# Two sums with x go from TensorE to VectorE at the end of a delta-rule and expert kernel

## The chip, the cores and the metric

The kernel runs on one core of one Trainium2 chip. The metric is the device time of one launch in microseconds (us). A core has TensorE (PE in the profile), VectorE (DVE), ScalarE (ACT), GpSimd (POOL) and SyncE (SP), which here only issues DMAs. TensorE multiplies out of SBUF into PSUM banks; GpSimd works on SBUF alone in this kernel.

## The reference

The input x is 2 sequences of 2048 tokens of width 256. It is normalised, and from the result two things are made: s, the output of a delta-rule attention with 4 heads, and g, the silu of a top-1 mixture of 8 experts. The output is x + s * g.

```python
xn = layernorm(x)
# s: delta rule, per head; q, k, v, beta are products with xn
def step(S, inp):
    q_t, k_t, v_t, b_t = inp
    pred = einsum('bhk,bhkv->bhv', k_t, S)
    delta = (v_t - pred) * b_t[..., None]
    S = S + k_t[..., :, None] * delta[..., None, :]
    return S, einsum('bhk,bhkv->bhv', q_t, S)
o = o * rsqrt(mean(o * o, -1) + EPS) * norm_w
o = o * (g_attn * sigmoid(g_attn))
s = o.reshape(b, n, H * DV) @ Wo
# g: each token goes through the one expert that its router chose
h = square(relu(einsum('btd,edh->ebth', xn, expert_fc)))
g = silu(sum over e of one_hot * einsum('ebth,edh->ebtd', h, expert_proj))
return x + s * g
```

## The kernel before, in words

The tokens are cut into 16 chunks of 128 tokens for both sequences, numbered 0 to 15. Each engine has its own list of steps, written out by hand: `ramp()`, a loop of `step3` and `step2`, and `tail()`. An engine runs its list strictly in that order; a step first waits on the semaphores of what it needs. So an early step that waits holds up everything behind it on that engine, and nothing on another engine unless that one waits for it.

The experts' part works on 39 tiles of sorted tokens. Its rows are scattered into a DRAM buffer `y_d` and, when all are there, loaded back into `wts` in four DMAs; the view of it for chunk c is `chunk_of(c)`. The output of chunk c is then made in place in two operations:

- `weigh(c)` on VectorE (L1839) multiplies `chunk_of(c)` by s, which lies in the buffer of `xT`.
- The sum with x is made in one of two ways. On TensorE, `add_x(c)` (L733 and L735) multiplies x and the chunk by the identity into one PSUM bank, and `keep_sum(c)` on ScalarE (L1225) copies the bank back. On VectorE, `add_x(c)` (L1844) is one addition. The list `ON_PE` names the chunks of the first kind.

SyncE then sends the 16 chunks out, strictly in the order 0 to 15 (L395), each once its sum is there.

The attention of the last chunk, 15, ends in a chain through four engines: `oss_(15)` and `og_(15)` on VectorE (L1816, L1810), `orn_(15)` and `ogm(15)` on GpSimd (L2424, L2426 and L2432), which scale `og` and signal `og_ok`; `ogT_(15)`, four transposes on TensorE (L710), that wait for `og_ok`; `ogTc(15)` on ScalarE (L1216), which copies them out of PSUM; `wo(15)` on TensorE (L722), the product with Wo, which needs that copy; `s_cp(15)` on ScalarE (L1221); and then `weigh(15)`, `add_x(15)` on VectorE and the last output DMA. These are the ends of the lists of TensorE and of VectorE, with the sums of the chunks put between the links.

```python
def added(c):
    return sum(1 for n in range(c + 1) if (n in ON_PE) == (c in ON_PE))
...
for c in range(NCH):
    sp.wait_ge(out_act if c in ON_PE else out_dve, added(c))
    sp.dma_start(o_v[c], chunk_of(c)).then_inc(o_out, 16)
```

Of the kernel before, what the change touches and what calls it, by code (L numbers as in the profile page):

```python
# [66 lines left out]
def build_program(nc, x, wq, wk, wvg, wbr, wo, norm_w, fc, pj, out):  # L67
    with ExitStack() as ctx:
# [203 lines left out]
        rank_ps = psum[RANK_BANK][:, 0:NQ * E]  # L272
        rows_ps = psum[LG_BANK][:, 0:2 * NT].rearrange("p (z j) -> p z j", z=2)

        ON_PE = [0, 2, 4, 6, 8, 9, 10, 11]

        def added(c):

            return sum(1 for n in range(c + 1) if (n in ON_PE) == (c in ON_PE))

        def sum_bank(c):
            return psum[H_BANK[added(c) % 2]][:].rearrange("p (b d) -> p b d", b=B)
# [31 lines left out]
        def chunk_of(c):  # L314
            return yf[:, c].rearrange("p (b d) -> p b d", b=B)

        def x_of(c):
            return (x_first[:, c] if c < NCH // 2 else x_last[:, c - NCH // 2]).rearrange("p (b d) -> p b d", b=B)
# [4 lines left out]
        with nc.Block() as block:  # L323
            @block.sync
            def _(sp):
# [67 lines left out]
# [3 lines that stand above are left out]
# [3 lines left out]
            def _(pe):  # L399
# [303 lines left out]
                def ogT_(c):  # L703
                    ch = At(pe, c)
                    ch.on(og_ok)
                    if c + 1 < NCH:
                        ch.stage(3, 0, S_ok)
                    for b in range(B):
                        for k in range(KC):
                            ins = pe.transpose(psum[CH_BANK][:, (b * KC + k) * P:(b * KC + k + 1) * P],  # L710
                                               og[:, H * b + 2 * k:H * b + 2 * k + 2, :].rearrange("p h n -> p (h n)"),
                                               ident[:])
                    ins.then_inc(ogTp, 1)
# [12 lines left out]
                def add_x(c):  # L726
                    n = added(c)
                    if n == 1:
                        At(pe, NT - 1).on(y_ok)
                    if n > 2:  # L730
                        pe.wait_ge(out_act, n - 2)
                    pe.wait_ge(xf_in[c // (NCH // 2)], 16 * B * GROUPS // 2)
                    pe.matmul(sum_bank(c), ident[:], x_of(c), start=True, stop=False)  # L733
                    pe.wait_ge(ys_ok, c + 1)
                    pe.matmul(sum_bank(c), ident[:], chunk_of(c), start=False, stop=True).then_inc(sum_ok, 1)  # L735
# [211 lines left out]
                def tail():  # L947
# [141 lines left out]
                    add_x(6)  # L1089
                    add_x(8)  # L1090
                    add_x(9)
                    add_x(10)
                    ogT_(15)
                    add_x(11)
                    wo(15)

                ramp()
# [4 lines left out]
            def _(act):  # L1102
# [40 lines left out]
                def relu(j, n):  # L1143
                    At(act, j).on(hp[n])
                    act.activation(half(n), psum[H_BANK[j % 2 ^ n]][:], ACT.Relu).then_inc(relu_ok[n], 1)  # L1145
# [20 lines left out]
                def ksq_(a, b):  # L1166
                    fr = At(act, a)
                    fr.on(Kp[b])
                    fr.on(Pl_ok[b], back=1)
                    act.activation(h4(f32_t, b), bank4(KG_BANK[b]), ACT.Square).then_inc(ksq[b], 1)  # L1170
# [52 lines left out]
                def keep_sum(c):  # L1223
                    act.wait_ge(sum_ok, SUM_FROM + added(c))
                    act.copy(chunk_of(c), sum_bank(c)).then_inc(out_act, 1)  # L1225
# [186 lines left out]
                def tail():  # L1412
                    ksq_(14, 0)
                    M0c(13, 1)
                    M0c(13, 0)
                    ksq_(14, 1)
                    osq(12)
                    relu(34, 0)
                    sq(34, 0)
                    q_h(14, 0)  # L1420
                    relu(34, 1)
                    sq(34, 1)
                    dZ(13, 0, 0)
                    dZ(13, 0, 1)
                    keep_rows(35)
                    dZ(13, 1, 0)
                    dZ(13, 1, 1)
                    keep_y(34)
                    q_h(14, 1)
                    dZ(13, 2, 0)  # L1430
                    dZ(13, 2, 1)
                    relu(35, 0)
                    sq(35, 0)
                    ogTc(12)
                    kTc(14, 1)
                    kTc(14, 0)
                    dZ(13, 3, 0)
                    dZ(13, 3, 1)
                    sig(14, 0)
                    relu(35, 1)  # L1440
                    sq(35, 1)
                    y_sigmoid(34)
                    dZ(13, 4, 0)
                    dZ(13, 4, 1)
                    s_cp(12)
                    keep_rows(36)
                    dZ(13, 5, 0)
                    dZ(13, 5, 1)
                    keep_y(35)
                    dZf_(13, 0)  # L1450
                    dZf_(13, 1)
                    sig(14, 1)
                    ksq_(15, 0)
                    ksq_(15, 1)
                    relu(36, 0)
                    M0c(14, 0)
                    M0c(14, 1)
                    osq(13)
                    sq(36, 0)
                    q_h(15, 0)  # L1460
                    relu(36, 1)
                    dZ(14, 0, 0)
                    sq(36, 1)
                    dZ(14, 0, 1)
                    kTc(15, 1)
                    dZ(14, 1, 0)
                    dZ(14, 1, 1)
                    keep_rows(37)
                    keep_y(36)
                    kTc(15, 0)  # L1470
                    q_h(15, 1)
                    relu(37, 0)
                    y_sigmoid(35)
                    dZ(14, 2, 1)
                    dZ(14, 2, 0)
                    sq(37, 0)
                    relu(37, 1)
                    ogTc(13)
                    dZ(14, 3, 0)
                    dZ(14, 3, 1)  # L1480
                    sq(37, 1)
                    M0c(15, 0)
                    M0c(15, 1)
                    keep_rows(38)
                    s_cp(13)
                    dZ(14, 4, 0)
                    dZ(14, 4, 1)
                    keep_y(37)
                    relu(38, 0)
                    y_sigmoid(36)  # L1490
                    dZ(15, 0, 0)
                    dZ(15, 0, 1)
                    sq(38, 0)
                    dZ(14, 5, 0)
                    y_sigmoid(37)
                    dZ(14, 5, 1)
                    dZ(15, 1, 1)
                    dZ(15, 1, 0)
                    relu(38, 1)
                    dZf_(14, 0)  # L1500
                    sig(15, 0)
                    dZf_(14, 1)
                    sq(38, 1)
                    dZ(15, 2, 1)
                    dZ(15, 2, 0)
                    keep_y(38)
                    y_sigmoid(38)
                    osq(14)
                    dZ(15, 3, 0)
                    dZ(15, 3, 1)  # L1510
                    sig(15, 1)
                    dZ(15, 4, 0)
                    dZ(15, 4, 1)
                    ogTc(14)
                    s_cp(14)
                    dZ(15, 5, 0)
                    dZ(15, 5, 1)
                    keep_sum(0)
                    dZf_(15, 0)
                    dZf_(15, 1)  # L1520
                    keep_sum(2)
                    osq(15)
                    keep_sum(4)
                    keep_sum(6)
                    keep_sum(8)
                    keep_sum(9)
                    keep_sum(10)
                    ogTc(15)
                    keep_sum(11)
                    s_cp(15)  # L1530

                ramp()
# [4 lines left out]
            def _(dve):  # L1537
# [296 lines left out]
                def weigh(c):  # L1834

                    dve.wait_ge(yf_in[c // CG], 16)
                    At(dve, c).on(s_ok)
                    y = chunk_of(c)
                    dve.tensor_tensor(y, y, s_all[:, 2 * c:2 * c + 2, :], ALU.mult).then_inc(ys_ok, 1)  # L1839

                def add_x(c):
                    dve.wait_ge(ys_ok, c + 1)
                    dve.wait_ge(xf_in[c // (NCH // 2)], 16 * B * GROUPS // 2)
                    dve.tensor_tensor(chunk_of(c), chunk_of(c), x_of(c), ALU.add).then_inc(out_dve, 1)  # L1844
# [232 lines left out]
                def tail():  # L2077
# [180 lines left out]
                    weigh(10)  # L2258
                    add_x(7)
                    weigh(11)  # L2260
                    weigh(12)
                    weigh(13)
                    add_x(12)
                    weigh(14)
# [334 lines left out]
```

## Time and profile before

| | |
|---|---|
| Time, median of 3 runs | 796.43 us (795.91 to 798.44) |
| The profiled execution | 795.13 us, with a span of 793.1 us and 2.03 us around it |
| Busy share of the span | PE 97%, PE weight load 82%, DVE 67%, POOL 49%, ACT 44% |
| Granted TensorE clock | 0.996 on average |

The span runs from the first to the last instruction that the profiler saw. A busy TensorE is not a TensorE at its peak. What the shares say is an average over 793 us; the change is in the last 16 us, and that stretch has its own limits.

### The profile page before, as it was taken

Reading aid. Unit: us, or ns where it says so; the run is one execution under the profiler, and the core shown is the slowest. Engines: PE = TensorE matmul, PEld = TensorE weight load, DVE = VectorE, ACT = ScalarE, POOL = GpSimd, SP = SyncE. Lnnn points to the kernel's source line nnn. Section 1 sums busy time; section 2 is a strip of 40 time slices with the busy share of each in tenths; the row PEclk is TensorE's granted clock in tenths of the full one; section 3 lists DMA queues with packets and bytes.
Section 4 is the critical chain, followed back from the end, with each engine's and each line's share of the span. In section 5 each row is a group of like instructions: output and inputs, shape, how many; then the busy total and the mean of one; then the engine's idle time right before and its main releaser. Section 6 shows DMA issues by size and latency. Waiting matters only on the chain.

```text
span 793.1 us, 22201 instructions
## 1 busy us (share of the span) xinstructions
PE 769.4 (97%) x9002; PEld 649.5 (82%) x9002; DVE 527.5 (67%) x1151; ACT 349.3 (44%) x762; POOL 389.7 (49%) x407
## 2 busy tenths in 40 slices
PE   6988999999999999999999999999999999999987
PEld 5957988888888888889888887888788887879854
DVE  6695475575655657556575667776777767777786
ACT  4713534454444543445344453444444444435432
POOL 3815363553635436354463546546463646545341
PEclk9999999999999999999999999999999999999999
DMA  8508832533335433363333632414142323323075
GB/s 298 195 27 335 330 141 114 196 138 147 128 114 206 151 124 127 114 240 121 120 127 124 229 115 86 156 30 175 45 138 104 128 108 127 128 107 114 9 248 197
DMA packets 37748, 116.25 MB, mean 147 GB/s; under 512 B 3664, under 2 KB 24400, under 8 KB 27664
## 3 DMA queue, kind: packets, MB, share of 16 engines
q1 hardware_dynamic: 33904, 104.62, 36.2%
q0 software_dynamic: 3744, 10.23, 3.9%
q8 instruction: 72, 1.18, 0.6%
q14 instruction: 28, 0.23, 0.1%
HBM read 101.33 MB, written 13.50 MB: 145 GB/s over the span
## 4 chain that ended last, share of the span: by engine, by line
PE 78%; DVE 8%; POOL 6%; issue 4%; DMA 3%; SPq 0%; ACT 0%; DVEq 0%; POOLq 0%
PE bank L504 18%; PE bank L515 16%; PE bank L548 6%; PE bank L533 5%; PE bank L580 5%; PE bank L478 3%; PE bank L480 3%; PE bank L479 3%; PE bank L620 2%; PE bank L722 2%; PE bank L638 2%; PE bank L629 2%; POOL XTl L2398 2%; PE bank L560 2%; POOL ImM L2418 2%
## 5 line engine op out<-in xcount | busy, mean ns | idle before, releaser
L515 PE MATMUL bank<-wts,hT 128*128 128x256 f32 x624 | 170.9, 393 | 0.0
L504 PE MATMUL bank<-xsT,wts 128*128 128x128 f32 x1248 | 166.0, 281 | 0.4 <-ACT xsT L1154 0.3
L504 PEld LDWEIGHTS bank<-xsT,wts 128*128 128x128 f32 x1248 | 150.5, 192 | 11.2 <-issue 11.1
L1761 DVE TENSOR_TENSOR Pm<-bank,lvl_mask 128x256 f16<-128x256 f32 x180 | 68.2, 418 | 67.1 <-PE bank L620 66.3
L515 PEld LDWEIGHTS bank<-wts,hT 128*128 128x128 f32 x624 | 105.4, 191 | 7.3
L2398 POOL TENSOR_TENSOR XTl<-f_t,XTh 128x512 f16<-128x512 f32 x32 | 39.9, 1253 | 137.0 <-DVE XTh L1701 136.9
L1772 DVE TENSOR_TENSOR M<-bank,M 128x256 f16<-128x256 f32 x180 | 68.8, 418 | 53.7 <-PE bank L629 53.2
L1200 ACT CAST Z<-bank 128x256 f16<-128x256 f32 x180 | 59.3, 376 | 99.9 <-PE bank L638 99.8
L1145 ACT ACTIVATE hT<-bank 128x512 f32<-128x512 f32 x78 | 46.7, 599 | 49.1 <-PE bank L504 49.1
L548 PE MATMUL bank<-xT,wq_sb 128*128 128x128 f32 x512 | 63.3, 277 | 0.4 <-DVE qT16l L1706 0.4
L580 PE MATMUL bank<-wvg_sb,xT 128*128 128x512 f32 x128 | 63.2, 617 | 0.0
L533 PE MATMUL bank<-wk_sb,xT 128*128 128x512 f32 x128 | 62.3, 613 | 0.3 <-ACT xT L1119 0.3
L548 PEld LDWEIGHTS bank<-xT,wq_sb 128*128 128x128 f32 x512 | 60.2, 192 | 0.9 <-issue 0.5
L2418 POOL TENSOR_TENSOR ImM<-ident,M 128x512 f32<-128x512 f16 x30 | 35.1, 1188 | 42.6 <-DVE M L1772 42.6
L1149 ACT ACTIVATE hT<-hT 128x512 f32<-128x512 f32 x78 | 49.4, 633 | 1.1
L2392 POOL TENSOR_TENSOR k16l<-f_t,k16h 128x512 f16<-128x512 f32 x32 | 37.9, 1199 | 22.3 <-DVE k16h L1687 22.3
L2371 POOL TENSOR_TENSOR y_sb<-y_sb,y_sg 128x256 f32<-128x256 f32 x39 | 29.5, 757 | 39.3 <-ACT y_sg L1164 39.2
L629 PEld LDWEIGHTS bank<-Pm,Z 128*128 128x128 f16 x720 | 32.8, 98 | 18.3 <-issue 11.4
L1694 DVE TENSOR_TENSOR f_t<-bank,up_neg 128x512 f32<-128x512 f32 x32 | 21.9, 685 | 37.8 <-PE bank L480 37.8
L2375 POOL DMA_INDIRECT y_d<-y_sb,to_row x39 | 41.0, 1052 | 8.6 <-issue 5.5
L2362 POOL DMA_INDIRECT xs<-xn_d,from_row x39 | 40.4, 1035 | 6.8 <-issue 5.9
L2349 POOL TENSOR_TENSOR root<-beta,up_half 128x8 f32<-128x8 f32 x16 | 29.3, 1829 | 29.1 <-DVE gate L1720 16.8
(247 smaller groups left out, 1956.4 us busy)
## 6 DMA issues: line engine op xcount, KB each, us to landing
wts<-in_fc SPq DMA_DIRECT2D x39, 1024.0 KB, 4.9
wts<-in_pj SPq DMA_DIRECT2D x39, 1024.0 KB, 8.1
wts<-in_x SPq DMA_DIRECT2D x10, 512.0 KB, 7.2
wts<-y_d SPq DMA_DIRECT2D x4, 1024.0 KB, 9.5
out_x<-wts SPq DMA_DIRECT2D x16, 256.0 KB, 2.3
xn_d<-wts SPq DMA_DIRECT2D x3, 1024.0 KB, 5.0
x_first<-in_x SPq DMA_DIRECT2D x4, 512.0 KB, 17.6
wts<-in_x SPq DMA_DIRECT2D x4, 256.0 KB, 3.5
```

The lines of the kernel that those rows point to most:

```text
L504: ins = pe.matmul(psum[bank[n]][:, (c % 4) * P:(c % 4 + 1) * P], fcw[r][:, k, c * P:(c + 1) * P], xsT[:, k, :], start=(k == 0), stop=(k == ...
L515: ins = pe.matmul(psum[bank[0]][:, 0:D], hT[:, c, :], pjw[r][:, c, :], start=(c == 0), stop=(c == HC - 1))
L533: ins = pe.matmul(psum[KG_BANK[b]][:], xT[:, a, b, k, :], wk_sb[:, k, :], start=(k == 0), stop=(k == KC - 1))
L548: ins = pe.matmul(bank4(QV_BANK)[:, h, :], wq_sb[:, k, h * DK:(h + 1) * DK], xT[:, a, b, k, :], start=(k == 0), stop=(k == KC - 1))
L580: ins = pe.matmul(psum[QV_BANK][:], xT[:, a, b, k, :], wvg_sb[:, k, :], start=(k == 0), stop=(k == KC - 1))
L629: ins = pe.matmul(half4(level_bank(m, b))[:, h, :], Zs[last(m)][:, H * b + h, :], Pms[last(m)][:, H * b + h, :], start=True, stop=True)
L1149: act.activation(half(n), half(n), ACT.Square).then_inc(sq_ok[n], 1)
L1200: act.copy(evens(h4(Zs[last(m)], b), s, 1), half4(level_bank(m, b)).rearrange("p h (n c) -> p h n c", c=s)).then_inc((last_dZ_ok if last(m ...
L1761: dve.tensor_tensor(h4(Pms[last(m)], b).rearrange("p h (n c) -> p h n c", c=s), half4(level_bank(m, b)).rearrange("p h (n c) -> p h n c", ...
L1772: dve.tensor_tensor(evens(h4(Ms[last(m)], b), s), half4(level_bank(m, b)).rearrange("p h (n c) -> p h n c", c=s), evens(h4(Ms[last(m)], b) ...
L2398: pool.tensor_tensor(h4(XT[1][a % 2], b), h4(f32_t, b), h4(XT[0][a % 2], b), ALU.subtract).then_inc(Xl_ok[b], 1)
L2418: pool.tensor_tensor(h4(ImM, b), ident16[:].unsqueeze(1).to_broadcast([P, H, P]), h4(Ms[last(m)], b), ALU.subtract).then_inc(ImM_ok[b], 1)
```

## The change

`ON_PE` loses chunks 10 and 11. On TensorE the two pairs of products for them go, one from ahead of `ogT_(15)` and one from between `ogT_(15)` and `wo(15)`; on ScalarE the two copies go; on VectorE two additions come in, the one behind `weigh(11)`, the other behind `weigh(12)`. SyncE's list is the same but for the semaphore on which chunks 10 and 11 wait.

```diff
-        ON_PE = [0, 2, 4, 6, 8, 9, 10, 11]
+        ON_PE = [0, 2, 4, 6, 8, 9]
...
                     add_x(9)
-                    add_x(10)
                     ogT_(15)
-                    add_x(11)
                     wo(15)
...
                     keep_sum(9)
-                    keep_sum(10)
                     ogTc(15)
-                    keep_sum(11)
                     s_cp(15)
...
                     weigh(11)
+                    add_x(10)
                     weigh(12)
+                    add_x(11)
                     weigh(13)
```

TensorE, the end of its list, before. L733 and L735 are the two products of one sum (`ident` is the identity), L710 the transposes, L722 the output product:

```order
L733 MATMUL bank<-wts,ident 128x512
L735 MATMUL bank<-wts,ident 128x512
L733 MATMUL bank<-wts,ident 128x512
L735 MATMUL bank<-wts,ident 128x512
L710 MATMUL bank<-ident,og 128x128 x4
L733 MATMUL bank<-wts,ident 128x512
L735 MATMUL bank<-wts,ident 128x512
L722 MATMUL bank<-wo_sb,ogT 128x256 x4
```

TensorE, the same place of the changed kernel:

```order
L733 MATMUL bank<-wts,ident 128x512
L735 MATMUL bank<-wts,ident 128x512
L710 MATMUL bank<-ident,og 128x128 x4
L722 MATMUL bank<-wo_sb,ogT 128x256 x4
```

One sum fewer stands ahead of the transposes, and nothing is left between them and the output product.

VectorE, the end of its list from `og_(15)` (L1810) on, before. L1839 is a `weigh`, L1844 an `add_x`:

```order
L1810 TENSOR_TENSOR og<-bank,gate 128x512
L1839 TENSOR_TENSOR wts<-wts,xT 128x512
L1844 TENSOR_TENSOR wts<-wts,x_first 128x512
L1839 TENSOR_TENSOR wts<-wts,xT 128x512 x3
L1844 TENSOR_TENSOR wts<-wts 128x512
L1839 TENSOR_TENSOR wts<-wts,xT 128x512
L1844 TENSOR_TENSOR wts<-wts 128x512 x2
L1839 TENSOR_TENSOR wts<-wts,xT 128x512
L1844 TENSOR_TENSOR wts<-wts 128x512
```

VectorE, the same place of the changed kernel, where every line number is 4 lower (L1806 is `og_(15)`, L1835 a `weigh`, L1840 an `add_x`):

```order
L1806 TENSOR_TENSOR og<-bank,gate 128x512
L1835 TENSOR_TENSOR wts<-wts,xT 128x512
L1840 TENSOR_TENSOR wts<-wts,x_first 128x512
L1835 TENSOR_TENSOR wts<-wts,xT 128x512
L1840 TENSOR_TENSOR wts<-wts 128x512
L1835 TENSOR_TENSOR wts<-wts,xT 128x512
L1840 TENSOR_TENSOR wts<-wts 128x512
L1835 TENSOR_TENSOR wts<-wts,xT 128x512
L1840 TENSOR_TENSOR wts<-wts 128x512
L1835 TENSOR_TENSOR wts<-wts,xT 128x512
L1840 TENSOR_TENSOR wts<-wts 128x512 x2
L1835 TENSOR_TENSOR wts<-wts,xT 128x512
L1840 TENSOR_TENSOR wts<-wts 128x512
```

Between `og_(15)` and the last `weigh` there are two more additions, and all else stands in the same order.

## Rows read from the trace of the kernel before

**Rows 1.** The page's head and its busy time by engine.

```profile
span 793.1 us, 22201 instructions
PE 769.4 (97%) x9002; PEld 649.5 (82%) x9002; DVE 527.5 (67%) x1151; ACT 349.3 (44%) x762; POOL 389.7 (49%) x407
```

**Rows 2.** The chain that ended last, from 784 us: start, us, what.

```profile
784.46 0.44 PE bank L710 x4
...
786.62 1.74 PE bank L722 x8
...
788.38 0.59 ACT xT L1221
...
789.07 0.70 DVE wts L1839
...
789.79 0.69 DVE wts L1844
```

**Rows 3.** SyncE's issues of output chunks 11 and 15.

```profile
787.26 0.37 SPq L395 DMA_DIRECT2D out_x<-wts  x1
...
790.51 0.37 SPq L395 DMA_DIRECT2D out_x<-wts  x1
```

**Rows 4.** Timeline of TensorE: start, us, engine, line, op [idle before].

```profile
782.58 1.02 PE L733 MATMUL bank<-wts,ident 128*128 128x512 f32 x2
...
784.30 0.60 PE L710 MATMUL bank<-ident,og 128*128 128x128 f32 x4
784.73 1.02 PE L733 MATMUL bank<-wts,ident 128*128 128x512 f32 x2
...
786.45 1.89 PE L722 MATMUL bank<-wo_sb,ogT 128*128 128x256 f32 x8
```

**Rows 5.** Timeline of GpSimd and of ScalarE ahead of the transposes.

```profile
781.32 1.45 POOL L2432 TENSOR_TENSOR og<-og,orn 128x512 f32<-128x512 f32 x1
...
782.78 0.58 ACT L1225 COPY wts<-bank 128x512 f32<-128x512 f32 x1 [1.13 <-PE bank L735]
```

**Rows 6.** Timeline of VectorE from 781 us.

```profile
781.18 0.68 DVE L1839 TENSOR_TENSOR wts<-wts,xT 128x512 f32<-128x512 f32 x1
781.78 1.53 DVE L1839 TENSOR_TENSOR wts<-wts,xT 128x512 f32<-128x512 f32 x1
783.24 0.68 DVE L1839 TENSOR_TENSOR wts<-wts,xT 128x512 f32<-128x512 f32 x1
783.84 0.68 DVE L1844 TENSOR_TENSOR wts<-wts 128x512 f32<-128x512 f32 x1
784.44 0.68 DVE L1839 TENSOR_TENSOR wts<-wts,xT 128x512 f32<-128x512 f32 x1
785.04 1.28 DVE L1844 TENSOR_TENSOR wts<-wts 128x512 f32<-128x512 f32 x2
789.07 0.69 DVE L1839 TENSOR_TENSOR wts<-wts,xT 128x512 f32<-128x512 f32 x1 [2.75 <-ACT xT L1221]
```

**Rows 7.** The same links for chunk 14, and one wait of TensorE on VectorE.

```profile
761.18 0.64 PE L710 MATMUL bank<-ident,og 128*128 128x128 f32 x4
...
761.85 0.58 ACT L1216 COPY ogT<-bank 128x512 f32<-128x512 f32 x1
...
770.91 0.68 DVE L1794 TENSOR_TENSOR R_l<-ru,R_h 128x512 f16<-128x512 f32 x1
...
771.74 0.19 PE L478 MATMUL bank<-R_h,wk_sb 128*128 128x64 f16 x1 [0.89 <-DVE R_l L1794]
```

**Rows 8.** GpSimd's scaling over all 16 chunks: ns min/median/max.

```profile
L2432 POOL TENSOR_TENSOR og<-og,orn x16: 1041/1042/1450, 120.1 to 781.3; 128x512 f32<-128x512 f32 x16
```

**Rows 9.** Stretches: busy by engine (PE, PEld, DVE, ACT, POOL), PEclk, DMA share, GB/s.

```profile
762.00:768.00 6.00, 4.53 (x69) 3.87 (x68) 5.29 (x9) 1.67 (x4) 2.97 (x3) 1.00 1.06 353
...
790.50:791.00 0.50, 0.00 (x0) 0.00 (x0) 0.00 (x0) 0.00 (x0) 0.00 (x0) 0.73 0.99 346
```

**Rows 10.** Timeline of TensorE, its longest idle time in that first stretch.

```profile
766.16 0.29 PE L638 MATMUL bank<-ident,wk_sb 128*128 128x64 f16 x4 [1.16 <-DVE wk_sb L1772]
```

## The prediction

> **What bounds the kernel now.** I read the page first. TensorE is busy for 97% of the span of 793.1 us [rows 1], so work taken from TensorE looks valuable. But the removed work lies in the last 16 us, and a share over the whole span says nothing about what ends last there. So the second view was the end of the chain that ended last. It goes from the output product `wo(15)` on TensorE to the copy `s_cp(15)` on ScalarE, to `weigh(15)` and `add_x(15)` on VectorE, and out by DMA [rows 2]. The last output DMA is issued at 790.51 us, and the span ends 2.59 us later [rows 3, 1].
>
> The third view was the timeline of each engine over those last 16 us. It shows two things. TensorE runs without a gap through the sums for chunk 10 (from 782.58), the transposes (784.30), the sum for chunk 11 (784.73) and `wo(15)` (786.45) [rows 4]. What the transposes need was there long before: GpSimd's last scaling of `og` ran from 781.32 for 1.45 us, so to 782.77, 1.53 us before they ran [rows 5, 4]. Here TensorE's order is what ends last. VectorE, in contrast, ended its queue at 786.32 (785.04 + 1.28) and then sat idle for 2.75 us until `s_cp(15)` was done [rows 6]. The reader is to see a slack of 2.75 us on the one engine and none on the other.
>
> **The TensorE side, step by step.** The sums for 10 and 11 take 1.72 us each: 784.30 - 782.58, and 786.45 - 784.73 [rows 4]. Removing both could bring at most 3.44 us. Two waits take part of that back.
>
> - The sum of chunk 9 ends where that of 10 began, at 782.58 [rows 4]. The transposes now wait for GpSimd, whose result is there at 782.77 [rows 5]. A wait of TensorE on another engine costs about 0.15 us: VectorE ended at 771.59 (770.91 + 0.68) and TensorE went on at 771.74 [rows 7]. So the transposes start at 782.92. For chunk 14 they took 0.64 us [rows 7], which gives 783.56.
> - ScalarE copies them out. It has ended the copy of sum 9 at 783.36 (782.78 + 0.58) and is free [rows 5]. For chunk 14 the copy began 0.03 us after the transposes' end (761.85 against 761.82) and took 0.58 [rows 7]: 783.59 to 784.17. Before, the sum of chunk 11 ran on TensorE during this copy and hid it; now TensorE idles. That is the new wait of this change, about 0.76 us with 0.15 us to start again, and only `wo(15)` is queued behind it.
> - `wo(15)` runs from 784.32 for 1.89 us [rows 4], to 786.21. `s_cp(15)` began 0.04 us after it (788.38 against 788.34) and took 0.59, and `weigh(15)` began 0.10 us after that (789.07 against 788.97) [rows 2, 4]. So `weigh(15)` could start at 786.94 instead of 789.07, which is 2.13 us earlier.
>
> **The VectorE side.** Operations of this shape that follow each other start 0.60 us apart (783.24, 783.84, 784.44, 785.04 [rows 6]), although each row says 0.68: they overlap a little. The two new additions have the same shape and engine as the four `add_x` that read `wts`, so they cost 2 x 0.60 = 1.20 us. They wait for nothing: chunks 10 and 11 are weighed ahead of them in VectorE's own list. Without them the slot for `weigh(15)` would be at 786.24 (785.04 + 2 x 0.60); with them it is 787.44. That is 0.50 us after the 786.94 at which s is ready. So VectorE becomes the bound of the last stretch, and of TensorE's 2.13 us, 1.63 us are left (789.07 - 787.44).
>
> At this place a rule speaks against the change and has to be weighed. One VectorE row is 1.53 us long instead of 0.68: `weigh(12)` at 781.78, right while GpSimd's scaling ran, which itself took 1.45 us against a median of 1.04 over 16 chunks [rows 6, 5, 8]. In the new order `add_x(10)` stands at 781.78 in place of `weigh(12)`, both read two operands from SBUF, so I carry the same 1.53 us over and add nothing. The Trainium skill, page "SBUF — State Buffer", section "SBUF: two separate sides", says that a VectorE operation with two SBUF inputs and a GpSimd operation that reads SBUF share a pair of ports under an exclusive lock, and the one that comes second waits for the whole of the other. By that rule too exactly one operation meets the scaling, and the sum would be the same; only a later GpSimd operation would change it, and after 782.77 there is none. Both rows agree with it.
>
> **SyncE and the output.** The issues stay in order. Chunk 11 went at 787.26 [rows 3], held up by TensorE and ScalarE, and 12 to 14 jammed behind it, although VectorE had ended them at 786.32. Now 11 can go once it is added, at about 784.6 (783.84 + 0.68), and chunk 14 at about 787.6: its addition takes the slot at 786.84, 1.20 us later than before. No transfer is left in front of the last one, where before the DMA engines were still 0.99 busy in the half microsecond after its issue [rows 9]. I leave the 2.59 us from the last issue to the end of the span as it is; should part of it have been queueing, the gain grows by up to about 0.5 us, that half microsecond.
>
> **The sum.** The last issue comes at 788.88 instead of 790.51, the span ends at 791.47. Against the profiled execution's own 795.13 us this is 793.50. That execution lies 1.30 us under the median of the runs shown, 796.43, so the predicted time is 796.43 - 1.63 = 794.8 us, or 0.2% less. A measurement of this kernel can tell about 0.3%, here 2.39 us, from no change. So this is a gain that a trace shows and a stopwatch hardly does.
>
> **The rivals.**
>
> - *The VectorE slot doesn't bind (gain 2.1 us or a little more, 794.3; chance 0.10).* It would, if additions packed tighter, or if the queueing in front of the last transfer goes. Against it: four starts in a row are 0.60 us apart [rows 6]. At 2.13 us plus some of the 0.5 us it would just pass the bound of 2.39.
> - *TensorE's clock falls in the new gaps (no gain, 796.5; chance 0.04).* The granted clock is 1.00, its level of 2.4 GHz, in all of 762 to 768, although TensorE sat idle for 1.16 us there, and it fell only after 790.5, two microseconds past the last product [rows 9, 10]. The new gaps are some 0.35 and 0.76 us. At half the clock the transposes and `wo(15)` would take 0.44 + 1.74 us more (both as the chain has them [rows 2]), `weigh(15)` would come at about 789.1, and the gain is gone.
> - *Slower: the additions on VectorE cost as much as the longest row (796.5; chance 0.04).* If both new additions took the 1.46 us from start to start that `weigh(12)` had (783.24 - 781.78) [rows 6], `weigh(15)` would slide to 786.24 + 2.92 = 789.16, 0.09 us later than before; it decides from 1.42 us each on. With one such addition the slot is 788.30 and the gain 0.77 us (795.7). For it speaks that VectorE would now be full up to its last operation; against it that GpSimd has nothing left to run and that nothing else in these rows stretched one [rows 6].
> - *The change does nothing to the end (796.4; chance 0.07).* This would be so if another chain, hidden now, ended at about 793 anyway, such as the output queue. Issues 12 to 14 followed on chunk 11 alone, so I see none.
> - *As forecast, between 1.2 and 2.0 us of gain; chance 0.75.*
>
> **How the numbers follow.** The cases run from 2.6 us of gain (2.13 + 0.5, 793.8) to 0.1 us of loss (796.5). The runs shown of one kernel spread from 0.5 us under to 2.0 us over their median, which is more than the effect. I take 793.7 to 796.6. Faster by over 0.3% needs 2.39 us, which only the first rival together with luck of the runs gives: 0.10. Slower by over 0.3% needs a loss that no case here gives, only scatter: 0.03. The rest, 0.87, is within 0.3%.
>
> **What the new profile would show.** Right: transposes at 782.9, with TensorE idle for about 0.35 us before them and about 0.8 us before `wo(15)`; `s_cp(15)` ended at about 786.8; VectorE without a gap from `oss_(15)` to the end of `add_x(15)`, about 788.85; the last issue at 788.9; all before 782 as it was. Wrong: an idle VectorE in front of `weigh(15)`; a second VectorE row well over 0.68 us after 783.3; a granted clock under 1.00 during `wo(15)`; or a last issue that lands later than 2.6 us.

## The result and the profile after

The changed kernel takes 794.67 us (median of 6 runs, 794.06 to 796.41), the kernel before 797.82 us (6 runs, 795.91 to 798.44). The ratio is 0.9972, with a 95% interval of 0.9962 to 0.9982: 2.2 us less, between 1.4 and 3.0. A second measurement of the unaltered changed kernel gave 0.9979 (0.9968 to 0.9990). Each ratio is to runs of the kernel before that were taken together with those of the changed one, and not to the 796.43 us of the first three runs. The forecast was 794.8 us, a ratio of 0.9980.

The two profiles differ by 0.8 us in the span:

```profile
span 792.3 us, 22185 instructions
PE 765.0 (97%) x8994; PEld 647.4 (82%) x8994; DVE 528.3 (67%) x1153; ACT 348.8 (44%) x760; POOL 390.1 (49%) x407
```

TensorE is busy 4.4 us less than in [rows 1] and its share is still 97%, so that share tells nothing of the change. The stretch to read is the last one. In this profile all of it lies 0.90 us later than in that of before (`og` is scaled from 782.21 instead of 781.32 [rows 5]), because of an idle time further up that the same code shows in one profile and not in another (`before_again`, below). So times are best counted from the start of `oss_(15)` on VectorE, the last step of chunk 15's chain that is at the same place in both: 778.18 before, 779.08 after. Timeline of TensorE, its weight loads (PEld), GpSimd and ScalarE, after:

```profile
782.62 1.02 PE L735 MATMUL bank<-wts,ident 128*128 128x512 f32 x2
783.72 0.66 PE L710 MATMUL bank<-ident,og 128*128 128x128 f32 x4
783.72 0.42 PEld L710 LDWEIGHTS bank<-ident,og 128*128 128x128 f32 x4 [0.90 <-POOL og L2430]
785.05 1.99 PE L722 MATMUL bank<-wo_sb,ogT 128*128 128x256 f32 x8 [0.67 <-ACT ogT L1214]
...
782.21 1.45 POOL L2430 TENSOR_TENSOR og<-og,orn 128x512 f32<-128x512 f32 x1
...
784.41 0.59 ACT L1214 COPY ogT<-bank 128x512 f32<-128x512 f32 x1
787.08 0.59 ACT L1219 COPY xT<-bank 128x512 f32<-128x512 f32 x1 [2.08 <-PE bank L722]
```

The sum of chunk 9 is now the last thing ahead of the transposes, and it ends in time, at 783.64. What they wait for is GpSimd: they start at 783.72, 0.06 us after it is done (783.66), and their weight load names it as its releaser. In the row of TensorE's products this wait is a gap of only 0.08 us. Between them and `wo(15)` TensorE stands idle for 0.67 us until ScalarE has copied. Where [rows 4] had one unbroken row, there are now two waits. Timeline of VectorE, after:

```profile
782.08 0.68 DVE L1835 TENSOR_TENSOR wts<-wts,xT 128x512 f32<-128x512 f32 x1
782.68 1.53 DVE L1840 TENSOR_TENSOR wts<-wts 128x512 f32<-128x512 f32 x1
784.14 0.68 DVE L1835 TENSOR_TENSOR wts<-wts,xT 128x512 f32<-128x512 f32 x1
...
787.15 1.28 DVE L1840 TENSOR_TENSOR wts<-wts 128x512 f32<-128x512 f32 x2
788.35 0.68 DVE L1835 TENSOR_TENSOR wts<-wts,xT 128x512 f32<-128x512 f32 x1
789.07 0.69 DVE L1840 TENSOR_TENSOR wts<-wts 128x512 f32<-128x512 f32 x1
```

`weigh(15)`, at 788.35, has no idle time in front of it, where [rows 6] had 2.75 us. Its input, the copy by ScalarE, was ready at 787.67. The operation that meets GpSimd's scaling is now `add_x(10)`, and it is 1.53 us long as `weigh(12)` was. The end of the chain that ended last shows the same:

```profile
787.22 0.50 DVE wts L1840
...
787.75 0.08 DVE wts L1840
787.83 0.52 issue
788.35 0.69 DVE wts L1835
789.04 0.02 issue
789.07 0.69 DVE wts L1840
```

("issue" is time in which the engine waited for nothing that the profile shows.) In [rows 2] this chain came from `wo(15)` and ScalarE; now it comes down VectorE's own queue. The last output DMA is issued at 789.78.

Counted from the start of `oss_(15)`, in us:

| kernel | transposes | `wo(15)` | ScalarE's copy done | `weigh(15)` | end of span | ratio to before (95%) |
|---|---|---|---|---|---|---|
| before | 6.12 | 8.27 | 10.79 | 10.89 | 14.92 | 1 |
| forecast for the change | 4.74 | 6.14 | 8.66 | 9.26 | 13.29 | 0.9980 |
| changed | 4.64 | 5.97 | 8.59 | 9.27 | 13.22 | 0.9972 (0.9962 to 0.9982) |
| only10 | 4.65 | 6.86 | 9.37 | 9.48 | 13.51 | 0.9981 (0.9970 to 0.9992) |
| only11 | 6.12 | 7.44 | 10.06 | 10.16 | 14.13 | 0.9998 (0.9989 to 1.0007) |
| drop12 | 4.64 | 5.97 | 8.58 | 8.69 | 12.72 | 0.9971 (0.9958 to 0.9984) |
| nine_too | 4.64 | 5.97 | 10.27 | 10.37 | 14.36 | 0.9991 (0.9981 to 1.0000) |
| nine_filled | 5.81 | 7.08 | 9.69 | 9.87 | 13.85 | 0.9982 (0.9972 to 0.9991) |
| after_yield | 4.64 | 5.97 | 8.58 | 9.44 | 13.45 | 0.9979 (0.9969 to 0.9989) |

Each entry is a start in that kernel's timeline less the start of its `oss_(15)`; the forecast's are its times less 778.18.

### The profile page after: what moved, and what is told of

It reads as the page before. It is cut to its first block, busy times and chain, and to the rows that moved or that the text cites. A ratio compares the mean times of both kernels' runs of the same rounds, so it can differ in the third digit from the quotient of the medians.

```text
span 792.3 us, 22185 instructions
## 1 busy us (share of the span) xinstructions
PE 765.0 (97%) x8994; PEld 647.4 (82%) x8994; DVE 528.3 (67%) x1153; ACT 348.8 (44%) x760; POOL 390.1 (49%) x407
## 3 DMA queue, kind: packets, MB, share of 16 engines
q8 instruction: 72, 1.18, 0.6%
## 4 chain that ended last, share of the span: by engine, by line
PE 80%; DVE 8%; issue 5%; POOL 5%; DMA 1%; another core or an unknown queue 0%; ACT 0%; DVEq 0%; POOLq 0%; SPq 0%
PE bank L504 18%; PE bank L515 15%; PE bank L548 7%; PE bank L533 6%; PE bank L580 5%; PE bank L480 4%; PE bank L478 3%; PE bank L479 3%; PE bank L620 2%; PE bank L638 2%; PE bank L629 2%; PE bank L722 2%; POOL XTl L2396 2%; PE bank L560 2%; POOL ImM L2416 2%
```

## The experiments

Each diff is against the changed kernel, unless it says otherwise.

**after_again: the changed kernel, unaltered.**

> The changed kernel once more, unaltered, to see how well its gain is known. Theory (TensorE's order gave 2.1 us, VectorE's queue took 0.5 back): the end of the program, counted from the start of oss_(15), is again 13.2 us away where it was 14.9 before, and the time is 1.7 us, or 0.2%, under that of the kernel before. Rival (the measured 0.28% holds more than this stretch, something earlier in the program): the time is 2.2 us or more under, with the stretch no shorter than 13.2. The idle time of VectorE at 683.7 us, 1.4 us longer than before in the first profile, is expected to be away if it is chance, and there again if the changed list brings it.

Measured: 795.03 us, ratio 0.9979; `weigh(15)` at 9.27 and the end at 13.30 after `oss_(15)`. The stretch repeats to 0.1 us, and the time agrees with the 1.6 us that the stretch gives (14.94 in `before_again` less 13.30). The idle time at about 684 us was there again; `before_again`, below, has more on it.

**only10: the sum of chunk 11 stays on TensorE.**

```diff
-        ON_PE = [0, 2, 4, 6, 8, 9]
+        ON_PE = [0, 2, 4, 6, 8, 9, 11]
...
                     ogT_(15)
+                    add_x(11)
                     wo(15)
...
                     weigh(12)
-                    add_x(11)
                     weigh(13)
```

> Only chunk 10's sum goes to VectorE; that of chunk 11 stays on TensorE, between the transposes and the output product. Theory: the transposes start when GpSimd is done, 4.6 us after the start of oss_(15), the output product follows 2.15 us later at 6.8, weigh(15) at 9.4 with VectorE idle for 0.1 to 0.2 us in front of it: gain 1.5 us, nearly the whole gain of the change, since the sum of chunk 11 stood in a gap that is needed anyway and its removal only exposed VectorE's queue. Rival (the two sums share the gain equally): weigh(15) at 10.0, gain 0.8 us.

VectorE's last operations in this kernel:

```profile
786.56 1.28 DVE L1842 TENSOR_TENSOR wts<-wts 128x512 f32<-128x512 f32 x2
788.57 0.69 DVE L1837 TENSOR_TENSOR wts<-wts,xT 128x512 f32<-128x512 f32 x1 [0.72 <-ACT xT L1220]
789.29 0.69 DVE L1842 TENSOR_TENSOR wts<-wts 128x512 f32<-128x512 f32 x1
```

`weigh(15)` came at 9.48, so 1.41 of the 1.62 us of the whole change. VectorE again waits for ScalarE, for 0.72 us; I had expected 0.1 to 0.2 there, because I set its freed slot at the changed kernel's 9.27 and not 0.60 us sooner. About half of the sum of chunk 11 stands in a gap that TensorE has anyway while ScalarE copies: with it `wo(15)` starts at 6.86 and without it at 5.97, so of its 1.72 us only 0.89 delay the chain. Of these VectorE's longer queue takes most again, and moving the sum adds 0.21 us of gain.

**only11: the sum of chunk 10 stays on TensorE.**

```diff
-        ON_PE = [0, 2, 4, 6, 8, 9]
+        ON_PE = [0, 2, 4, 6, 8, 9, 10]
...
                     add_x(9)
+                    add_x(10)
                     ogT_(15)
...
                     weigh(11)
-                    add_x(10)
                     weigh(12)
```

> Only chunk 11's sum goes to VectorE; that of chunk 10 stays on TensorE, ahead of the transposes. Theory: transposes at 6.1 us after the start of oss_(15) as before, the copy to ScalarE waits for the copy of sum 10 until 6.8, the output product at 7.5, weigh(15) at 10.2 with VectorE idle in front of it, so 0.7 us earlier than the 10.9 of before: gain 0.7 us. Rival (a removed sum is worth its 1.72 us of TensorE): weigh(15) at 9.2, gain 1.7 us.

`weigh(15)` came at 10.16, a gain of 0.73 us, and the time is that of before within its interval. With the sum of 10 ahead of them, the transposes stay at 6.12, and the removed 1.72 us of TensorE are worth less than half. The two sums are not additive either: 0.73 and 1.41 alone, 1.62 together.

**drop12: one operation less on VectorE.** It leaves out the sum with x of chunk 12; SyncE then waits for `weigh(12)` alone.

```diff
...
                     weigh(13)
-                    add_x(12)
                     weigh(14)
```

> The changed kernel without the sum with x of chunk 12 on VectorE; that chunk is put out without x. This takes 0.60 us from VectorE's queue and nothing from the chain of chunk 15. Theory (VectorE's queue is what ends last in front of weigh(15)): weigh(15) comes 0.58 us earlier than in the changed kernel, 8.7 us after the start of oss_(15) instead of 9.27, and then waits for s_cp(15) by about 0.1 us; the end is at 12.6 instead of 13.2. Rival (the s chain is the bound and VectorE is only busy beside it): weigh(15) stays at 9.27.

`weigh(15)` came at 8.69, 0.58 us earlier, the end at 12.72, with nothing changed on TensorE or ScalarE (5.97 and 8.58). This shows that VectorE's queue is what ends last in the changed kernel, and what that costs.

**nine_too: the sum of chunk 9 goes to VectorE as well.**

```diff
-        ON_PE = [0, 2, 4, 6, 8, 9]
+        ON_PE = [0, 2, 4, 6, 8]
...
-                    add_x(9)
                     ogT_(15)
...
                     add_x(7)
+                    add_x(9)
                     weigh(11)
                     add_x(10)
```

> The changed kernel with the sum of chunk 9 on VectorE as well, ahead of the second last block of sums (behind add_x(7) and weigh(11)). Theory: TensorE's side can't gain, since the transposes wait for GpSimd at 4.64 us after the start of oss_(15), and VectorE's queue is 0.60 us longer: weigh(15) at 9.87, the end at 13.8 instead of 13.2, so 0.6 us of the gain is given back. Rival (sums on TensorE are what ends last): weigh(15) earlier than 9.27.

In the kernel that ran, `add_x(9)` stands between `add_x(7)` and `weigh(11)`, and not behind `weigh(11)` as the expectation has it; the queue is as long either way, and the operation that meets GpSimd's scaling is `weigh(11)` here.

`weigh(15)` came at 10.37, half a microsecond later than even the theory said. Timeline of TensorE, and stretches of this kernel (busy time by engine, PEclk, DMA share, GB/s):

```profile
784.18 0.66 PE L710 MATMUL bank<-ident,og 128*128 128x128 f32 x4 [1.79 <-POOL og L2429]
785.51 3.68 PE L722 MATMUL bank<-wo_sb,ogT 128*128 128x256 f32 x8 [0.68 <-ACT ogT L1213]
```

```profile
784.00:786.00 2.00, 1.15 (x5) 0.86 (x6) 2.00 (x4) 0.59 (x1) 0.12 (x1) 0.90 0.95 322
786.00:788.00 2.00, 2.00 (x6) 1.61 (x5) 2.00 (x4) 0.00 (x0) 0.00 (x0) 0.50 0.68 232
```

The row to see is `wo(15)` with 3.68 us instead of 1.99, at a granted clock of 0.50, 1.2 GHz. TensorE had been idle for 1.79 and, after the short transposes, for 0.68 us. This is the clock rival of the prediction. It did not come in the changed kernel, but it comes one sum further, and costs 1.69 us on `wo(15)`.

**nine_filled: the same with the gap filled.** The diff is against nine_too.

```diff
                     add_x(8)
+                    At(pe, 15).on(gate_ok[1])
+                    for _ in range(14):
+                        pe.matmul(psum[QV_BANK][:, 0:P], ident[:], ident[:], start=True, stop=True)
                     ogT_(15)
```

> The kernel with chunk 9's sum on VectorE too, and 14 products of the identity with itself into a bank that nobody reads, on TensorE in the gap ahead of the transposes. In the unfilled kernel TensorE was idle there for 1.79 us, its granted clock then fell to 0.50, and wo(15) took 3.68 us. Theory (the fall of the clock made wo(15) slow and not the order of the sums): the clock stays at 1.00, wo(15) takes 1.99 us, weigh(15) comes at 9.87 us after oss_(15), when VectorE's queue allows it, instead of 10.37, and the end is at 13.8 instead of 14.36. Rival (wo(15) is slow in this order anyway): it stays at 3.7 us.

The same two views:

```profile
781.03 3.29 PE L1093 MATMUL bank<-ident 128*128 128x128 f32 x28
784.16 0.60 PE L710 MATMUL bank<-ident,og 128*128 128x128 f32 x4
785.43 1.99 PE L722 MATMUL bank<-wo_sb,ogT 128*128 128x256 f32 x8 [0.67 <-ACT ogT L1216]
```

```profile
784.00:786.00 2.00, 1.33 (x10) 1.03 (x10) 2.00 (x5) 0.58 (x1) 0.00 (x0) 1.00 0.71 246
```

The clock stays at 1.00 and `wo(15)` takes 1.99 us. The filling was too long, 3.29 us, and held the transposes up to 5.81. Even so `weigh(15)` came at 9.87, to the hundredth where VectorE's queue puts it: 9.27 + 0.60. So useless products that delay the transposes by 1.2 us win 0.5 us, since the clock was worth 1.7.

**before_again: the kernel before, a second profile.**

> The kernel before, unaltered, for a second profile. All four changed kernels profiled so far show VectorE idle for 2.5 to 2.6 us after S32_ at about 684 us, with no releaser recorded, and reach chunk 13 about 1.0 us later than the first profile of before. If this stall belongs to the changed lists, this profile has only the 1.0 us wait on TensorE there, and the gain of the change in the time would be 1.7 - 1.0 = 0.7 us. If the first profile of before was the exception, this one has the 2.5 us stall too, oss_(15) starts at about 779.3 instead of 778.2, and the time of the change is 1.7 us under that of before.

796.21 us, ratio 0.9998. `weigh(15)` is at 10.89 and the end at 14.94 after `oss_(15)`, as in the first profile. The long idle time is not there, and `oss_(15)` starts at 778.76, so neither branch came out whole. The version `weigh_early` below decides: of its two profiles the second shows the idle time and the first not, with the same code. So the changed lists don't bring it by themselves: of the twelve profiles of kernels other than before, six have it. That before never has it rests on two profiles alone. VectorE around it in `before_again` and in the changed kernel:

```profile
685.41 0.75 DVE L1761 TENSOR_TENSOR Pm<-bank,lvl_mask 128x256 f16<-128x256 f32 x2 [0.98 <-PE bank L620]
```

```profile
686.27 0.76 DVE L1757 TENSOR_TENSOR Pm<-bank,lvl_mask 128x256 f16<-128x256 f32 x2 [2.56 <-remote]
```

**weigh_early: the changed kernel with VectorE's idle time used.** VectorE stands idle for 1.18 us in front of `oss_(15)`, while ScalarE squares.

```diff
                     add_x(5)
-                    oss_(15)
                     weigh(9)
-                    og_(15)
                     weigh(10)
+                    oss_(15)
+                    og_(15)
                     add_x(7)
```

> The changed kernel with weigh(9) and weigh(10) moved ahead of oss_(15), into the 1.18 us in which VectorE waits for the square of the last output. Theory (VectorE's queue is what ends last in front of weigh(15)): counted from the start of the square on ScalarE (9.90 us to weigh(15) in the changed kernel), weigh(15) comes 0.58 us earlier, at 9.3, and ends waiting for s_cp(15) by about 0.1 us; time 0.6 us under the changed kernel, 2.3 us under before. Risk: if the two operations reach past the square's end, oss_(15) and with it the transposes slide by the same amount. Rival (VectorE's order doesn't matter): weigh(15) stays at 9.9.

> The version with weigh(9) and weigh(10) ahead of oss_(15) once more, unaltered, since its first measurement (ratio 0.9963) rests on five runs. Counted from R_l(15), weigh(15) started at 15.7 us and the span ended at 19.8, where the changed kernel has 16.5 and 20.5 and before has 18.2 and 22.2. Theory (the gain is what that stretch shows): the same two numbers again, and a time 2.4 us under before, a ratio of 0.997. If the first ratio held chance from elsewhere in the program, this one lies nearer to 0.998.

The ratios are 0.9963 (0.9950 to 0.9977) and 0.9966 (0.9954 to 0.9978): 2.7 to 2.9 us under before, the fastest version of all, though its interval still overlaps that of the changed kernel. VectorE in the first profile:

```profile
788.55 0.69 DVE L1835 TENSOR_TENSOR wts<-wts,xT 128x512 f32<-128x512 f32 x1 [0.30 <-ACT xT L1219]
789.28 0.69 DVE L1840 TENSOR_TENSOR wts<-wts 128x512 f32<-128x512 f32 x1
```

Counted from `R_l(15)` (772.84 there, 771.81 in the changed kernel), `weigh(15)` comes at 15.71 instead of 16.54 and the end at 19.76 instead of 20.49; the second profile has 15.71 and 19.71. It is 0.83 us and not the 0.58 expected, because the transposes came 0.24 us sooner as well (4.40 instead of 4.64 after `oss_(15)`), and now VectorE waits 0.30 us for ScalarE. They came sooner because GpSimd did, for a reason that the prediction and the expectations had overlooked. Before:

```profile
778.94 0.58 POOL L2424 TENSOR_TENSOR orn<-oss,o_eps 128x8 f32<-128x8 f32 x1 [9.67 <-DVE oss L1816]
```

In `weigh_early`:

```profile
780.87 0.20 POOL L2422 TENSOR_TENSOR orn<-oss,o_eps 128x8 f32<-128x8 f32 x1 [9.66 <-DVE oss L1812]
```

This first operation of `orn_(15)` has a median of 0.20 us over the 16 chunks of before, but takes 0.58 us for chunk 15 there and in the changed kernel, where `weigh(9)`, with two operands in SBUF, runs beside it. In `weigh_early` it is `og_(15)` that runs beside it, which reads one operand from a PSUM bank, and the row is 0.20 us long. The same holds in every profile here: 0.58 us with a `weigh` beside it, 0.20 with `og_(15)`. So GpSimd meets VectorE twice in this chain. In `weigh_early` the scaling then began 2.76 instead of 3.13 us after `oss_(15)` and took 1.23 instead of 1.45 us; TensorE, still at the sum of chunk 9, let the transposes gain only 0.24 us of it.

**o_early: O(15) ahead of the sum of chunk 4.**

```diff
-                    add_x(4)
                     O(15)
+                    add_x(4)
                     add_x(6)
                     add_x(8)
-                    add_x(9)
                     ogT_(15)
+                    add_x(9)
                     wo(15)
...
-                    keep_sum(9)
                     ogTc(15)
+                    keep_sum(9)
                     s_cp(15)
```

> The changed kernel with another order on TensorE: the output product O(15) ahead of the sum of chunk 4 instead of behind it, and the sum of chunk 9 behind the transposes, in the gap in front of wo(15). Theory: O(15) starts at its U_l, 1.1 to 1.2 us earlier, and with it the square, oss_(15), GpSimd and the transposes; VectorE's wait for the square of 1.18 us is gone, so its queue ends 1.2 us earlier. The sum of chunk 9 in the gap costs 0.9 us of that on TensorE, so wo(15) comes 0.4 us earlier than in the changed kernel, s is ready 0.9 us before the changed kernel's weigh(15), and the end is 0.9 to 1.0 us earlier than the changed kernel's; time 2.6 us under before. Rival (sums moved about on TensorE change nothing while VectorE is full): no more than 0.2 us against the changed kernel.

This was wrong by the sign: 800.94 us, a ratio of 1.0053 (1.0039 to 1.0067). Timeline of GpSimd, VectorE and TensorE:

```profile
781.88 6.27 POOL L2430 TENSOR_TENSOR og<-og,orn 128x512 f32<-128x512 f32 x1
...
781.76 0.67 DVE L1835 TENSOR_TENSOR wts<-wts,xT 128x512 f32<-128x512 f32 x1
782.36 0.67 DVE L1840 TENSOR_TENSOR wts<-wts 128x512 f32<-128x512 f32 x1
...
785.98 1.27 DVE L1840 TENSOR_TENSOR wts<-wts 128x512 f32<-128x512 f32 x2
...
788.21 0.99 PE L710 MATMUL bank<-ident,og 128*128 128x128 f32 x4 [4.92 <-POOL og L2430]
...
790.70 1.57 PE L735 MATMUL bank<-wts,ident 128*128 128x512 f32 x2
```

GpSimd's scaling of `og` takes 6.27 us where [rows 8] have a median of 1.04 and a largest of 1.45. No VectorE row is stretched this time: its queue of operations with two SBUF operands runs on at 0.60 us each and ends at 787.25; GpSimd ends 0.90 us later, at 788.15. TensorE waits 4.92 us for it, and then its clock is low too:

```profile
790.00:792.00 2.00, 2.00 (x4) 0.84 (x3) 0.00 (x0) 0.00 (x0) 0.00 (x0) 0.55 0.00 0
```

From the start of the transposes to that of `wo(15)` 3.90 us pass (788.21 to 792.11).

**o_early_yield: VectorE steps aside.** The diff is against o_early.

```diff
                     weigh(11)
+                    At(dve, 15).on(og_ok)
                     add_x(10)
```

> The kernel with O(15) ahead of the sum of chunk 4 took 6.27 us for GpSimd's scaling of og, which ended when VectorE's queue did. Here VectorE, behind weigh(11), first waits for that scaling. Theory (VectorE's unbroken row of operations that read two SBUF operands kept GpSimd out): the scaling takes 1.04 to 1.3 us, the transposes start at 4.2 to 4.4 us after oss_(15), weigh(15) comes at 9.2 after it, and the end is 19.2 to 19.5 us after R_l(15), where the changed kernel has 20.5 and before 22.2. Rival (GpSimd was slow for another reason): the scaling stays over 3 us.

One wait on VectorE brings the kernel from 800.94 to 793.92 us (ratio 0.9976, 0.9964 to 0.9988). The scaling takes 1.45 us, VectorE idles for 0.94. So it was VectorE's queue that kept GpSimd out. Counted from `oss_(15)`, `weigh(15)` comes at 9.45 here and at 15.96 in o_early: of these 6.5 us, 4.8 are the scaling itself (6.27 less 1.45), and 1.7 are TensorE's low clock behind it (2.21 us from the transposes to `wo(15)` here, with the same products between them, instead of 3.90). `weigh(15)` starts 15.47 us after `R_l(15)` (786.71 and 771.24), 1.07 us earlier than in the changed kernel, yet the span ends at 20.86 and not at 19.5. The rest was lost behind the last sum, in the output. SyncE's issues, and stretches of this kernel (columns as in [rows 9]):

```profile
784.91 0.37 SPq L395 DMA_DIRECT2D out_x<-wts  x1
...
787.67 0.71 SPq L395 DMA_DIRECT2D out_x<-wts  x1
788.43 0.73 SPq L395 DMA_DIRECT2D out_x<-wts  x1
```

```profile
787.00:788.00 1.00, 0.00 (x0) 0.00 (x0) 0.97 (x2) 0.00 (x0) 0.00 (x0) 1.00 1.03 345
788.00:789.00 1.00, 0.00 (x0) 0.00 (x0) 0.13 (x1) 0.00 (x0) 0.00 (x0) 0.65 1.04 337
```

Chunk 9, whose sum now comes late on TensorE, goes at 784.91, and the six behind it follow each other closely with longer and longer issues; the last takes 0.73 us instead of 0.37. It comes 0.99 us after the start of `add_x(15)` instead of 0.71, and from it to the end of the span 3.67 us pass (788.43 to 792.1) instead of 2.52, with the DMA engines full. That the late chunk 9 makes this, since it holds up the chunks behind it, is argued from the order of the issues; no run moves it alone.

**after_yield: the same wait in the changed kernel.**

> The changed kernel with the same wait of VectorE behind weigh(11). Theory (one operation of VectorE stood 1.53 us because it waited out the scaling): the scaling falls from 1.45 to 1.04 - 1.2 us since it has nobody to wait for but weigh(11), the next addition is 0.68 us long, the transposes come 0.2 to 0.4 us earlier, and weigh(15) stays within 0.2 us of its 9.27 us after oss_(15), since the idle time takes the place of the stretched operation. Rival (the stretched operation is slow by itself): it stays at 1.53 us.

```profile
781.35 0.68 DVE L1835 TENSOR_TENSOR wts<-wts,xT 128x512 f32<-128x512 f32 x1
782.97 0.69 DVE L1840 TENSOR_TENSOR wts<-wts 128x512 f32<-128x512 f32 x1 [0.94 <-POOL og L2431]
...
781.48 1.45 POOL L2431 TENSOR_TENSOR og<-og,orn 128x512 f32<-128x512 f32 x1
```

`add_x(10)` is 0.69 us long when it starts after the scaling, so the 1.53 us in the changed kernel were a wait inside the row. The scaling did not shrink, against what I expected: it stays at 1.45 us. It begins at 781.48 while `weigh(11)` runs, and 1.45 less the median of 1.04 leaves 0.41 us, about what `weigh(11)` still had to go until 781.95, where the next operation would have started. `weigh(15)` moved by 0.17 us.

## Why the prediction was right

- **TensorE's order ended last before, by 1.53 us over GpSimd.** Right. The transposes moved up by 1.48 us (6.12 to 4.64), which only10 shows to be the sum of chunk 10 alone.
- **Two waits take back part of the 3.44 us.** Right. The transposes started 0.06 us after GpSimd was done, where I had taken 0.15; the other wait was 0.67 us, where I had 0.76. `wo(15)` took 1.99 us instead of 1.89. ScalarE's copy was ready at 8.59 against 8.66 forecast.
- **VectorE becomes the bound and gives back 0.5 us.** Right, shown by drop12 from one side and nine_filled from the other. `weigh(15)` came at 9.27 against 9.26 forecast. What was given back is 0.58 us (9.27 - 8.69). Each term of the sum is within 0.1 us of its row; that ScalarE's copy comes within 0.07 us owes something to errors that offset, the two restarts 0.09 and 0.10 us too long and `wo(15)` 0.10 too short.
- **One operation meets GpSimd's scaling, whichever it is.** Right for the changed kernel (1.53 us, now on `add_x(10)`). But what I took from it, that the meeting costs the same however the order is changed, holds only while VectorE lets GpSimd in. o_early is the case in which it does not; against o_early_yield it costs 6.5 us, 4.8 in the scaling and 1.7 by TensorE's clock. And GpSimd is held up once more in this chain, at its first operation (0.58 instead of 0.20 us), which the prediction did not see. It is the same in both kernels and so left the forecast alone; weigh_early shows it.
- **The last DMA.** From the last issue to the end took 2.52 us (789.78 to 792.3) instead of 2.59, and in after_again 2.59 (790.11 to 792.7). So the possible gain of up to 0.5 us from an emptier queue did not come.
- **The size in the time.** The stretch gives 1.70 us (14.92 - 13.22), the forecast 1.63. The first measurement's 2.2 us holds this within its interval; the second, 0.9979, lies on it. The time itself, 794.67 against 794.8, is near by luck: the forecast started from 796.43, the median of three runs, and the kernel before came out at 797.82 in six; the gain was 0.6 us larger than forecast in the first measurement.
- **The rivals.** By the time alone the first rival, in which VectorE's slot doesn't bind (2.1 us of gain or a little more, 794.3), fits as well as the forecast; the profile rules it out, as `weigh(15)` has no idle time in front of it, and so does drop12. The end moved with `weigh(15)`, so no other chain held it at 793. The clock did not fall in gaps of about 0.1 and 0.67 us (1.00 in all of 784 to 788). nine_too shows how near it was: there, with 1.79 us of idle time in front of the transposes, it fell. I had priced both products at half clock and had it at 4 in 100; in the changed kernel that stands, for one more sum it would not. The full price on each addition did not come either: only one VectorE row was stretched, and the others started 0.60 us apart.

## What to carry to other kernels

Price a move from one engine to another at both ends: what the source's waits take back, and at what time the target's queue is through. Here 3.44 us of TensorE became 2.2 us at ScalarE's copy, 1.6 us at `weigh(15)` and 1.7 us at the end, and half of the move (only10) brought nearly all of it. Then look for idle time on the new bound ahead of the chain, and put work there that is ready (weigh_early).

A full queue on VectorE of operations that read two SBUF operands held GpSimd out for as long as it lasted in one order (o_early), and for one operation in the others. So where a chain passes through GpSimd beside such a queue, look at the length of GpSimd's row after every change of order. One wait on VectorE cured it in o_early; in the changed kernel, where there was nothing to cure, the same wait made `weigh(15)` 0.17 us later.

## What the runs showed of the hardware beyond this

- **GpSimd kept out.** The same scaling took 1.45 us in before, the changed kernel and nine_filled, against nearly the same row of VectorE operations, 1.23 in weigh_early, and 6.27 in o_early. In o_early and in the changed kernel GpSimd began 0.12 and 0.13 us after the start of a VectorE operation (781.88 and 781.76; 782.21 and 782.08), so the phase does not tell them apart. Nor does an earlier stop of VectorE: weigh_early had none in front of `oss_(15)` and GpSimd got in. What decides stays open. The Trainium skill, page "SBUF — State Buffer", section "SBUF: two separate sides", says that whichever starts first holds the shared ports for its whole instruction; the stretched rows agree, but in o_early eight operations of VectorE started after GpSimd and went first.
- **TensorE's clock early in the program.** It differs between profiles of the program's first part, which is the same in all versions: from 60 to 65 us the granted clock was 0.66 in weigh_early and 1.00 in the changed kernel, and from 55 to 60 it was 0.63 in weigh_early_2. First weigh_early, then the changed kernel (columns as in [rows 9]):

```profile
60.00:65.00 5.00, 5.00 (x62) 4.94 (x62) 2.63 (x12) 0.65 (x2) 3.51 (x3) 0.66 0.34 93
```

```profile
60.00:65.00 5.00, 4.16 (x65) 3.82 (x62) 4.09 (x16) 1.23 (x3) 4.04 (x3) 1.00 0.45 141
```

  From there on weigh_early ran 2.1 us behind the changed kernel (`og` of chunk 0 scaled at 122.03 and 119.95), and kept that distance up to 684 us. With the 1.0 us that the idle time there leaves, whose cause stays open, this is as large as the effect measured here, and it is why the time alone tells so little where the stretch is clear in one profile.
